# Moving and dropping the points at which GpSimd waits for VectorE while it scatters the edges of a graph

## The chip, the core and the metric

The kernel runs on one core of a Trainium2 chip. The metric is the device time of one execution in microseconds (us), lower is better. The kernel before takes 8104.89 us, the median of 3 runs (8100.04 to 8139.46). One more thing to keep in mind: the profile below was taken of the slowest of those three runs.

Engines are named as in the profile: PE is TensorE (PEld its weight load), DVE is VectorE, ACT is ScalarE, POOL is GpSimd, SP is SyncE. A small q behind the name, as in SPq, means the engine's own instruction queue.

## The reference, cut to what matters

Four graph layers run one after the other on 6250 nodes with 64 features and 206,250 directed edges, sorted by destination. Each is followed by a residual sum and a layer norm.

```python
edge_index = jnp.stack([src, dst])
x = _layernorm(x + _L0_gnn_ref(x, edge_weight, edge_weight_n2, ..., src, dst), axis=-1)
x = _layernorm(x + _L1_gnn_ref(x, edge_index, edge_attr_32, ...), axis=-1)
x = _layernorm(x + _L2_gnn_ref(x, edge_index, ...), axis=-1)
x = _layernorm(x + _L3_gnn_ref(x, edge_index, edge_attr_32, ...), axis=-1)

def _spmm(w, src, dst, h, n):
    return jax.ops.segment_sum(w[:, None] * h[src], dst, num_segments=n)
h_low = relu(_spmm(w_low, src, dst, x @ W_low, n))     # layer 0, and the same with w_high
seg_sum = segment_sum(edge_attr, row, num_segments=N)  # layer 1, with a maximum and a count too
```

Layers 0 and 1 need, for each edge, the features of its source and the edge's own 32 attributes, summed by destination or by source. The change lies in the stage that prepares this.

## The kernel before, in words

`build` runs `setup`, then `placing`, `grouping`, the rest of layer 0, and layers 1 to 3. Only `placing` is touched (lines 231 to 624).

`placing` takes the edges in NBK = 51 blocks of 4096 (128 partitions x 32 columns; the columns are c = 0 to 31). For each block it works out to which row of a table in DRAM, `pay_d`, each edge's record of 36 words goes. The table has one grid cell for each source node and block. An edge that finds its cell free goes there, the others go to a list of seconds. Then POOL scatters the records, one column of 128 rows for each call of `indirect_dma_start` (line 349), 32 calls for a block. Two blocks later the grid of a block is loaded back (line 311), and its messages are multiplied and summed into windows of 128 destinations.

The work is a pipeline over blocks, with three buffers of each kind (index j, block modulo 3). The first three blocks are written out, the other 48 run in a loop of 16 turns (`over_thirds`). All engines have the same loop and meet by semaphores alone. In stage b

- DVE compares the edges' numbers with a row of numbers (`hots(b)`, lines 501 to 506), adds up the window of block b-3 (`close_window`, 584 to 587), reads the loaded grid of block b-2 (`open_grid`, 551 to 560), and then makes the messages of block b-2 in NS = 7 parts u = 0 to 6 (`messages`, 565 to 572). Ahead of part 4 stands `ranks(b)` (512 to 522), ahead of part 6 `places(b)` (526 to 547), whose last instruction, L547, writes the row numbers of block b for POOL. `close_grid` (575 to 578) ends the stage.
- PE counts edges of block b in four batches (`counts`, 428 and 432), looks numbers up (`lookups`, 443), makes two totals (449, 450), and multiplies the messages of block b-2 part by part (`spread`, 457 to 462). Part 0 stands between batches 1 and 2, part 1 between batches 2 and 3, the others behind the lookups.
- ACT copies the end of each batch (376, 377), the running counts (382), and widens the marks of each part (370). At the end of its stage it issues three DMAs that clear other tables (398 to 400).
- SP loads a row, the edges' records and the fill of block b's grid (317 to 323), and then, when all 32 scatters of block b-2 have landed, the grid of block b-2 (311).
- POOL waits for block b's row numbers and issues its 32 scatters. Behind some of the columns it waits for a part of the messages: the table `behind` (line 338) says that ahead of column c it waits until `val_ready` has counted `(b - 1) * NS + behind[c]` parts. These are the parts of block b-1, which DVE makes in stage b+1.

Further waits on which the argument rests: part u waits in DVE for `sub_done` of part u-2 from PE (line 564), because the two buffers alternate. ACT's copy of batch t waits for PE's `batch_ready`. PE's part u waits for ACT's marks of part u.

Of the kernel before, what the change touches and what calls it, by code (L numbers as in the profile page):

```python
# [76 lines left out]
def over_thirds(eng, blocks, body):  # L77
    for b in range(3):
        body(b, 0, b)
    with eng.Fori(1, blocks // 3) as i:  # L80
        for j in range(3):
            body(i * 3 + j, i, j)
# [148 lines left out]
def placing(nc, z, k, a):  # L231
# [3 lines left out]
    with ExitStack() as ctx:  # L235
# [67 lines left out]
        with nc.Block() as block:  # L303
            @block.sync
            def _(sp):
                def load_grid(b, i, j):
                    sp.wait_ge(rows_out[j], i * (CB * 16) + CB * 16)
                    sp.sem_inc(starts, 1)
                    sp.wait_ge(grid_used, b + 1)
                    sp.sem_inc(starts, 1)  # L310
                    sp.dma_start(grid[j][:, :, :].rearrange("p s w -> p (s w)"),
                                 gv[at(b)].rearrange("b l w -> (b l) w")).then_inc(grid_in[j], 16)

                def stage(b, i, j):
                    wait(sp, lo_hot_ready, b)
                    sp.sem_inc(starts, 1)
                    sp.dma_start(lo_row[:, :], a["lo_d"][at(b), :].to_broadcast([P, BE])).then_inc(lo_in, 16)
                    wait(sp, rows_out[j], i * (CB * 16))
                    sp.sem_inc(starts, 1)
                    sp.dma_start(row[j][:, :, :].rearrange("p c w -> p (c w)"),  # L320
                                 a["pay"][at(b)].rearrange("b p w -> (b p) w")).then_inc(row_in[j], 16)
                    sp.dma_start(gv[at(b)].rearrange("b l w -> (b l) w"), fg).then_inc(filled[j], 16)
                    sp.dma_start(sv[at(b)].rearrange("b p w -> (b p) w"), fs).then_inc(filled[j], 16)
                    two_back(load_grid, b, i, j)

                over_thirds(sp, NBK, stage)
                load_grid(NBK - 2, NBK // 3 - 1, 1)
                load_grid(NBK - 1, NBK // 3 - 1, 2)
                for j in range(3):
                    sp.wait_ge(rows_out[j], NBK // 3 * (CB * 16))  # L330
                lv = sec_view(z, a)
                for j in range(3):
                    sp.dma_start(k.row[j][:, :, :].rearrange("p c w -> p (c w)"), lv[j]).then_inc(k.row_in[j], 16)
                sp.wait_ge(starts, 4 * NBK)

            @block.gpsimd
            def _(pool):
                behind = {17: 1, 20: 3, 23: 4, 26: 5, 29: 7}

                def stage(b, i, j):  # L340
                    pool.wait_ge(filled[j], i * 32 + 32)
                    pool.wait_ge(row_in[j], i * 16 + 16)
                    pool.wait_ge(place_ready, b + 1)
                    pool.sem_inc(k.pool_steps, 1)
                    for c in range(CB):
                        if c in behind and not (isinstance(b, int) and b < 1):
                            pool.wait_ge(val_ready, (b - 1) * NS + behind[c])
                            pool.sem_inc(k.pool_steps, 1)
                        pool.indirect_dma_start(a["pay_d"][:, :], bass.IndirectOffsetOnAxis(ap=place[j][:, c:c + 1], axis=0),  # L349
                                                row[j][:, c, :], None).then_inc(rows_out[j], 16)  # L350

                over_thirds(pool, NBK, stage)
                pool.wait_ge(lo_hot_ready, NBK)
                for j in range(3):
                    pool.wait_ge(k.row_in[j], 16)
                    for c in range(SC):
                        gather_listed(pool, k, a, j, c)
# [357 lines left out]
def gather_listed(pool, k, a, j, c):  # L715
    pool.indirect_dma_start(k.xs[j][:, c, :], None, a["x"][:, :],  # L716
                            bass.IndirectOffsetOnAxis(ap=k.row[j][:, c, AT_SRC:AT_SRC + 1].bitcast(i32), axis=0)
                            ).then_inc(k.x_in[j], 16)
# [2379 lines left out]
```

## Time and profile before

| | us |
|---|---|
| median of three runs | 8104.89 |
| the profiled execution's own time | 8139.46 |
| its span in the profile | 8137.8 |
| `placing`, the 32 x 51 scatters, first to last | 91.0 to 2897.4 |

The whole span has PE busy 63%, PEld 53%, DVE 57%, ACT 19% and POOL 54%. In the stretch of `placing` no engine is near full: it is a ring of waits between POOL, DVE, PE and ACT, and it has to be read from the times at which one engine lets another go. The rows that do so stand below. In a row of the timeline the number in brackets is the time for which the engine was idle before this instruction, and behind the arrow what ended it. "remote" stands where a semaphore's update ended the wait and no instruction of this core ended at that moment; "issue" where the profile shows no wait.

### The profile page before, as it was taken

Reading aid. Unit: us, or ns where it says so; the run is one execution under the profiler, and the core shown is the slowest. Engines: PE = TensorE matmul, PEld = TensorE weight load, DVE = VectorE, ACT = ScalarE, POOL = GpSimd, SP = SyncE. Lnnn points to the kernel's source line nnn. Section 1 sums busy time; section 2 is a strip of 40 time slices with the busy share of each in tenths; the row PEclk is TensorE's granted clock in tenths of the full one; section 3 lists DMA queues with packets and bytes.
Section 4 is the critical chain, followed back from the end, with each engine's and each line's share of the span. In section 5 each row is a group of like instructions: output and inputs, shape, how many; then the busy total and the mean of one; then the engine's idle time right before and its main releaser. Section 6 shows DMA issues by size and latency. Waiting matters only on the chain. (4 is left out here: it accounts for less than half of the span.)

```text
span 8137.8 us, 135968 instructions
## 1 busy us (share of the span) xinstructions
PE 5140.9 (63%) x47718; PEld 4318.4 (53%) x47719; DVE 4606.7 (57%) x8883; ACT 1556.5 (19%) x3166; POOL 4394.8 (54%) x4199
## 2 busy tenths in 40 slices
PE   2555555555555532235555567999995878778776
PEld 1433434434334422223455446999995666666665
DVE  4555555555555534445555465666665666666665
ACT  1111111111111110001111141000002333333332
POOL 3666565566566555552455554555552555555552
PEclk7677767766776766665666666999997888889887
DMA  4333233233233211111000130111113333333332
GB/s 132 112 126 126 100 123 124 102 123 126 100 123 126 86 44 28 28 29 13 21 22 22 26 120 21 27 26 26 26 25 90 95 100 95 99 98 100 95 96 52
DMA packets 303354, 621.11 MB, mean 76 GB/s; under 512 B 153436, under 2 KB 229902, under 8 KB 285521
## 3 DMA queue, kind: packets, MB, share of 16 engines
q1 hardware_dynamic: 153693, 405.75, 14.4%
q0 software_dynamic: 133216, 116.93, 6.6%
q10 hardware_dynamic: 15994, 92.31, 3.2%
q8 instruction: 297, 4.87, 0.2%
q14 instruction: 154, 1.26, 0.0%
HBM read 547.78 MB, written 235.06 MB: 96 GB/s over the span
## 5 line engine op out<-in xcount | busy, mean ns | idle before, releaser
L349 POOL DMA_INDIRECT pay_d<-row,place x1632 | 1711.9, 1049 | 1184.7 <-DVEq L572 646.0
L462 PE MATMUL win<-onehot,val 128*128 128x128 f32 x4998 | 881.9, 346 | 444.7 <-issue 233.4
L462 PEld LDWEIGHTS win<-onehot,val 128*128 128x128 f32 x4998 | 804.4, 251 | 628.7 <-issue 317.9
L2032 PE MATMUL g_win<-g_hot,y_part 128*128 128x128 bf16 x14994 | 867.8, 220 | 21.0 <-issue 11.4
L2012 POOL DMA_INDIRECT g_x<-xg_d,g_row x459 | 579.2, 1262 | 539.7 <-PE g_win L2032 413.0
L2032 PEld LDWEIGHTS g_win<-g_hot,y_part 128*128 128x128 bf16 x14994 | 847.1, 98 | 34.1 <-issue 17.2
L2534 POOL DMA_INDIRECT m_from_src<-from_src_d,m_row x459 | 515.4, 1123 | 630.6 <-PE m_pre L2570 430.7
L565 DVE TENSOR_TENSOR hot<-near_dve,drel 128x896 bf16<-128x896 bf16 x357 | 222.6, 624 | 1017.4 <-remote 746.3
L716 POOL DMA_INDIRECT lo_row_and_x<-in_x,r_row x459 | 436.9, 952 | 423.6 <-PEq L839 238.6
L1275 POOL DMA_INDIRECT sorted_d<-s_row,s_place x459 | 439.5, 958 | 333.8 <-DVE s_place L1391 145.4
L2537 POOL DMA_INDIRECT m_from_dst<-from_dst_d,m_row x459 | 518.8, 1130 | 139.9 <-issue 134.4
L832 PE MATMUL r_win<-r_onehot,r_val 128*128 128x160 f32 x918 | 212.6, 411 | 559.5 <-DVEq L856 551.3
L432 PE MATMUL pair<-hot_hi,hot_lo 128*128 128x392 bf16 (+3 forms) x1632 | 301.0, 350 | 409.2 <-DVE hot_hi L503 384.9
L832 PEld LDWEIGHTS r_win<-r_onehot,r_val 128*128 128x128 f32 x918 | 197.6, 278 | 584.1 <-DVEq L856 567.4
L2570 PEld LDWEIGHTS m_pre<-m_q_win,m_hot_t 128*128 128x128 bf16 x7497 | 358.6, 103 | 258.1 <-issue 191.7
L2570 PE MATMUL m_pre<-m_q_win,m_hot_t 128*128 128x64 bf16 x7497 | 401.5, 200 | 136.3 <-issue 135.5
L432 PEld LDWEIGHTS pair<-hot_hi,hot_lo 128*128 128x128 bf16 x1632 | 203.0, 131 | 535.8 <-issue 236.7
L2566 PE MATMUL m_pre<-m_w_four,m_ea_t 96*128 96x192 f32 (+1 forms) x1428 | 468.7, 409 | 16.7 <-issue 16.2
L370 ACT ACTIVATE onehot<-hot 128x896 f32<-128x896 bf16 x357 | 333.9, 951 | 669.3 <-DVE hot L565 612.7
L2711 DVE TENSOR_TENSOR m_hid<-m_pre,p_nodes 128x448 f32<-128x448 f32 x357 | 221.9, 622 | 404.0 <-remote 201.6
L2081 DVE TENSOR_TENSOR g_hot<-iota,g_drel 128x896 bf16<-128x896 f32 x364 | 374.5, 1087 | 110.9 <-PE g_win L2032 102.9
L2587 PE MATMUL m_win<-m_hot,m_parts 128*128 128x128 bf16 x2499 | 343.4, 229 | 68.1 <-DVE m_parts L2723 44.7
(455 smaller groups left out, 10646.9 us busy)
## 6 DMA issues: line engine op xcount, KB each, us to landing
m_hot_t<-drow_d SPq DMA_DIRECT2D x52, 1568.0 KB
scan_d<-in_none ACTq DMA_DIRECT2D x51, 1034.2 KB
lo_row_and_x<-lo_d SPq DMA_DIRECT2D x51, 1024.0 KB
m_grid<-pay_d SPq DMA_DIRECT2D x52, 882.0 KB
pay_d<-in_fill SPq DMA_DIRECT2D x51, 882.0 KB
grid<-pay_d SPq DMA_DIRECT2D x51, 882.0 KB
pay_d<-in_fill SPq DMA_DIRECT2D x51, 648.0 KB
sorted_d<-in_none ACTq DMA_DIRECT2D x51, 581.8 KB
```

The source lines that it names most:

```text
L349: pool.indirect_dma_start(a["pay_d"][:, :], bass.IndirectOffsetOnAxis(ap=place[j][:, c:c + 1], axis=0), row[j][:, c, :], None).then_inc(ro ...
L432: last = mm(pair[h][:, q, c * NT:BK * NT].rearrange("p (n s) -> p n s", s=NT), hot_lo[:, e, :], hot_hi[:, e, 0:NT].unsqueeze(1).to_broadca ...
L462: last = mm(win[:, :], val[u % 2][:, s, :], onehot[u % 2][:, s, :], start=(u == 0 and s == 0), stop=(u == NS - 1 and s == SUB - 1))
L716: pool.indirect_dma_start(k.xs[j][:, c, :], None, a["x"][:, :], bass.IndirectOffsetOnAxis(ap=k.row[j][:, c, AT_SRC:AT_SRC + 1].bitcast(i32 ...
L832: mm(win[j][:, :], val[j][:, c, :], onehot[j][:, c, :], start=(c == 0), stop=(c == SC - 1))
L1275: pool.indirect_dma_start(a["sorted_d"][:, :], bass.IndirectOffsetOnAxis(ap=place[j][:, c:c + 1], axis=0), row[j][:, c, :], None).then_inc ...
L2012: pool.indirect_dma_start(xs[j][:, c, :], None, a["xg_d"][:, :], bass.IndirectOffsetOnAxis(ap=row[j][:, c, AT_SRC:AT_SRC + 1].bitcast(i32) ...
L2032: last = mm(win[:, h, 0:W], k.y[q][:, t, h * P:(h + 1) * P], hot[u][:, s, :], start=(t == 0 and q == 0), stop=(t == NT - 1 and q == 2))
L2534: pool.indirect_dma_start(ps_x[j][:, c, :], None, a["from_src_d"][:, :], bass.IndirectOffsetOnAxis(ap=row[j][:, c, AT_SRC:AT_SRC + 1].bitc ...
L2537: pool.indirect_dma_start(qs_x[j][:, c, :], None, a["from_dst_d"][:, :], bass.IndirectOffsetOnAxis(ap=row[j][:, c, AT_DST:AT_DST + 1].bitc ...
L2566: mm(out[:, first * D:(first + size) * D], ea_t[u % 2][0:size * F, o:o + P], w_four[0:size * F, 0:size * D], start=True, stop=False)
L2570: last = mm(out[:, s * D:(s + 1) * D], hot_t[j][:, (u * SUB + s) * P:(u * SUB + s + 1) * P], q_win[j][:, q * D:(q + 1) * D], start=False, ...
```

## The change

The table `behind` of `placing` gets one entry less, and the others move three columns back:

```diff
@@ -335,7 +335,7 @@
 
             @block.gpsimd
             def _(pool):
-                behind = {17: 1, 20: 3, 23: 4, 26: 5, 29: 7}
+                behind = {20: 1, 23: 3, 26: 4, 29: 5}
 
                 def stage(b, i, j):
                     pool.wait_ge(filled[j], i * 32 + 32)
```

Before, POOL waits ahead of columns 17, 20, 23, 26 and 29 for 1, 3, 4, 5 and 7 parts. Now it waits ahead of columns 20, 23, 26 and 29 for 1, 3, 4 and 5 parts, and for all seven nowhere. The calls are the same 32 in the same order; PE, DVE, ACT and SP have the same instructions in the same order as before.

On POOL, in the loop, for the block with buffer 1 (`place_ready`, `filled1` and `row_in1` say that the row numbers are made, the grid is filled and the records are loaded; `val_ready` counts message parts; L347 and L343 are the waits' own register work):

```order
 L343 REGISTER_ALU [waits row_in1,filled1]
 L349 DMA pay_d<-row,place 554880x36 [waits place_ready]
-L349 DMA pay_d<-row,place 554880x36 x16
+L349 DMA pay_d<-row,place 554880x36 x19
 L347 ISA
-L349 DMA pay_d<-row,place 554880x36 [waits val_ready]
-L349 DMA pay_d<-row,place 554880x36 x2
-L347 REGISTER_ALU
 L349 DMA pay_d<-row,place 554880x36 [waits val_ready]
 L349 DMA pay_d<-row,place 554880x36 x2
```

The first wait for a part now stands behind 20 calls instead of 17, and one group of three calls with its wait is gone. The blocks with buffers 0 and 2 read alike.

## Rows read from the trace of the kernel before

**Rows 1.** Costliest groups: busy, mean ns of one, idle before and its releaser.

```profile
L349 POOL DMA_INDIRECT pay_d<-row,place x1632 | 1711.9, 1049 | 1184.7 <-DVEq L572 646.0
```

**Rows 2.** Busy time by stretch: PE, PEld, DVE, ACT, POOL, clock, DMA.

```profile
90.00:2900.00 2810.00, 1493.11 (x9150) 1115.18 (x9150) 1509.29 (x2650) 445.09 (x800) 1711.87 (x1632) 0.71 0.32 114
```

**Rows 3.** Waits of DVE from 90 to 2900: total us, times, longest.

```profile
DVE hot L565 <- remote: 736.0, 52, 18.8
DVE hot L565 <- PE win L462: 212.6, 57, 25.6
DVE dst_f L551 <- DMA grid<-pay_d: 123.2, 49, 6.2
```

**Rows 4.** Waits of POOL from 90 to 2900.

```profile
POOL pay_d L349 <- DVEq L572: 646.0, 154, 13.9
```

**Rows 5.** Timeline of POOL, 1605 to 1668: start, duration, instruction, idle before.

```profile
1605.94 0.97 POOL L349 DMA_INDIRECT pay_d<-row,place  x1 [0.31 <-issue]
1612.47 0.97 POOL L349 DMA_INDIRECT pay_d<-row,place  x1 [5.56 <-DVEq L572]
...
1619.12 0.96 POOL L349 DMA_INDIRECT pay_d<-row,place  x1 [3.14 <-DVEq L572]
...
1626.59 1.90 POOL L349 DMA_INDIRECT pay_d<-row,place  x1 [3.97 <-DVEq L572]
1628.80 0.97 POOL L349 DMA_INDIRECT pay_d<-row,place  x1 [0.31 <-issue]
1630.07 2.04 POOL L349 DMA_INDIRECT pay_d<-row,place  x1 [0.30 <-issue]
...
1661.15 0.96 POOL L349 DMA_INDIRECT pay_d<-row,place  x1 [0.30 <-issue]
1667.78 0.96 POOL L349 DMA_INDIRECT pay_d<-row,place  x1 [5.67 <-DVEq L572]
```

**Rows 6.** Timeline of DVE, 1609 to 1666.

```profile
1609.94 0.63 DVE L565 TENSOR_TENSOR hot<-near_dve,drel 128x896 bf16<-128x896 bf16 x1 [15.27 <-remote]
...
1623.95 0.19 DVE L547 TENSOR_TENSOR place<-away,pos 128x32 int32<-128x32 f32 x1
...
1625.13 0.61 DVE L570 TENSOR_TENSOR val<-x_nodes,near_dve 128x448 f32<-128x448 f32 x1
1625.87 1.79 DVE L575 TENSOR_TENSOR p_nodes<-grid,p_nodes 128x1568 f32<-128x1568 f32 x1
...
1629.47 1.79 DVE L578 TENSOR_TENSOR p_nodes<-p_nodes,tmp 128x1568 f32<-128x1568 f32 x1
...
1640.15 0.34 DVE L551 CAST dst_f<-grid 128x49 f32<-128x49 int32 x1 [3.04 <-DMA grid<-pay_d]
...
1647.95 0.61 DVE L570 TENSOR_TENSOR val<-x_nodes,near_dve 128x448 f32<-128x448 f32 x1
1665.25 0.62 DVE L565 TENSOR_TENSOR hot<-near_dve,drel 128x896 bf16<-128x896 bf16 x1 [16.69 <-remote]
```

**Rows 7.** Timeline of PE and ACT around three copies, and PE's part 1.

```profile
1581.78 1.67 PE L432 MATMUL pair<-hot_hi,hot_lo 128*128 128x392 bf16 x8
1583.49 0.21 ACT L376 ACTIVATE last_b<-pair 128x49 bf16<-128x49 f32 x1 [1.97 <-PE pair L432]
1592.43 0.99 PE L432 MATMUL pair<-hot_hi,hot_lo 128*128 128x392 bf16 x8
1598.67 0.21 ACT L376 ACTIVATE last_b<-pair 128x49 bf16<-128x49 f32 x1 [9.86 <-remote]
1601.74 1.31 PE L462 MATMUL win<-onehot,val 128*128 128x128 f32 x6
```

**Rows 8.** The same copy of ACT in another block, and POOL there.

```profile
1549.04 0.96 POOL L349 DMA_INDIRECT pay_d<-row,place  x1 [0.30 <-issue]
1550.51 0.21 ACT L376 ACTIVATE last_b<-pair 128x49 bf16<-128x49 f32 x1 [20.33 <-remote]
1557.64 0.97 POOL L349 DMA_INDIRECT pay_d<-row,place  x1 [7.64 <-DVEq L572]
```

**Rows 9.** Issue of a grid's load and of the clearing DMAs.

```profile
1625.38 0.84 ACTq L398 DMA_DIRECT2D sorted_d<-in_none  x1
1635.47 0.34 SPq L311 DMA_DIRECT2D grid<-pay_d  x1
```

**Rows 10.** The last block: POOL's last wait, and DVE's wait for its grid.

```profile
2893.89 1.91 POOL L349 DMA_INDIRECT pay_d<-row,place  x1 [1.71 <-DVEq L572]
2905.30 0.20 DVE L551 CAST dst_f<-grid 128x49 f32<-128x49 int32 x1 [5.47 <-DMA grid<-pay_d]
```

## The prediction, made before the changed kernel was run

> **What bounds the kernel now.** The page comes first. Its costliest group is the scatter of L349, 1632 calls, with 646.0 us of idle time ended by DVE's L572, which is exactly the wait that the change touches [rows 1]. Next the busy time of this stretch: of 2810 us POOL is busy 1711.87, DVE 1509.29, PE 1493.11 [rows 2]. Nobody is full, so the stretch is a ring of waits, and I read who lets whom go.
>
> DVE's longest wait is part 3 of the messages, ended by a "remote" update, 736.0 us in 52 times [rows 3]. The releaser should be PE's `sub_done`. In the block of rows 7 PE's part 1 ends at 1601.74 + 1.31 = 1603.05, yet DVE starts at 1609.94, 6.9 us later [rows 6]. PE's signal is held. The same shows at ACT: early in a run of scatters its copy starts at 1583.49, 0.04 us after PE's batch ends (1581.78 + 1.67), but later in that run it starts at 1598.67, 5.25 us after PE's end (1592.43 + 0.99) [rows 7].
>
> When is the held signal let go? POOL's last call before its pause ends at 1605.94 + 0.97 = 1606.91; DVE goes on at 1609.94, 3.03 us into the pause. In the next block POOL stops at 1661.15 + 0.96 = 1662.11 and DVE goes on at 1665.25, after 3.14 us [rows 5, 6]. So in both blocks PE's signal comes through only when POOL has stopped for about 3.1 us. POOL in turn stops only because it waits for that very part (column 23, four parts). That closes the ring: the length of a block is set by where POOL pauses, and by what it must wait for before its next long run.
>
> In the trace I count, for each of blocks 2 to 49, a pause ahead of columns 23, 26 and 29 and none ahead of 17 and 20: three a block, about 150 of the 154 waits [rows 4]. The block of rows 5 runs from 1606.91 to 1662.11, 55.20 us:
> - 5.56 us pause, three calls, 3.14 us pause, three calls: to 1626.59 it is 19.68 us.
> - then 26 calls in one go (columns 29 to 31, and 0 to 22 of the next block), 1626.59 to 1662.11, 35.52 us, three of them lengthened by DVE's instructions.
>
> **The change part by part.** Column 17's wait goes, and column 20 waits for one part instead of three. Neither ever made POOL idle, so both cost and give nothing. Column 23 now waits for three parts. The third is made at 1647.95 + 0.61 = 1648.56 [rows 6]; column 23 will be called some 8 us after that, by the sum below (three calls before 1606.91 + 53.6), so it does not pause either. The cover of that 8 us is the quick release of PE's part 0; were it held as well, this would be the pause.
>
> Column 26 takes over the wait for four parts and with it the long pause. The signal still comes 3.1 us after the stop, so I keep 5.56 us. Column 29 takes over the wait for five parts, 6.65 us after column 26 (1619.12 - 1612.47), since DVE's parts 3 and 4 lie so far apart whatever POOL does. So column 29 is called at 5.56 + 6.65 = 12.21 us after the stop, and its three calls end at 12.21 + 3 x 0.97 + 2 x 0.30 = 15.7.
>
> What is late next is `place_ready` of the following block, since the wait for seven parts is gone. L547 ends at 1624.14, and part 4's wait ended at 1619.12: 5.02 us. With the 0.85 us that POOL needs from DVE's end to its call (1625.13 + 0.61 = 1625.74 to 1626.59) [rows 5, 6], column 0 starts at 12.21 + 5.02 + 0.85 = 18.08. Then again 26 calls in one go (columns 0 to 25) with the same three long ones: 35.52 us. A block is 53.6 us instead of 55.2. The difference is simply part 6 end minus L547 end, 1625.74 - 1624.14 = 1.60 us, and I find this same distance in all 48 blocks.
>
> The scatters of a block now end earlier: before, column 31 ended at 1630.07 + 2.04 = 1632.11 and SP issued the grid's load at 1635.47. Now the last call ends at 1606.91 + 15.7 = 1622.6, and the load goes out near 1626, beside ACT's clearing DMAs (1625.38) [rows 9]. It took 4.7 us to DVE's L551 before, and DVE would be ready for it at 1637.1 (3.04 us before 1640.15). There are 11 us for it, enough even at twice the time. So DVE's wait for the grid, 123.2 us in 49 times, 2.5 each [rows 3], goes. I give it no gain: the two parts before the hold come 2.5 us sooner, and then DVE waits for part 3, which POOL's pause releases. That wait is what is late next. At the least it brings nothing, at the most its whole 2.5 us a block.
>
> The end of the stage: the last block paused 1.71 us at column 29, and DVE then waited 5.47 us for its grid [rows 10]. The pause for five parts moves back there by three calls (3.8 us) and the release with it. Of the 5.47 us I expect 1 to 3 to be won.
>
> Sum: 48 x 1.60 = 77, and about 3 for the end: 80 us. The profiled execution's 8139.46 becomes about 8060; from the median of 8104.89 it is **8025 us**, the profiled execution being the slowest of the three. Bounds of the unshown: the pause ahead of column 0, 2.4 us (15.7 to 18.1), may not clear what POOL has queued as 3.14 and 3.97 did. Below it costs nothing, above it costs what the slower rival says.
>
> Two rules of the Trainium skill, SBUF — State Buffer, section "SBUF: two separate sides". It says that on the engine side only the port pair shared by DVE and GpSimd causes contention, and that PE and ACT never wait for anyone. By that alone POOL's run could hold back nothing of PE's, and the long pause would not exist, before or after. The rows disagree (6.9 us held, let go 3.1 us after the stop), and I go by them. The same section says that the pair is an exclusive lock: whoever starts first has it for its whole instruction. POOL's calls do take 1.90 and 2.04 us where DVE's L575 and L578 run, against 0.97 otherwise. But L578 starts at 1629.47, within the call of 1628.80 to 1629.77, and keeps its 1.79 us, so the lock shows in one direction only. If calls of columns 0 to 2, now ahead of those instructions, did block DVE, it would lose up to 3 us of slack that it has before part 3, and the sum would stay.
>
> **The rivals.**
> - *The hold comes sooner and the change is slower.* POOL's 26 calls now start after a short pause of 2.4 us. If that does not clear its queue, PE's batches 1 and 2 (14 and 20 us into the run) are held earlier and longer. One block prices it: where batch 2 was held until POOL stopped, the pause ahead of column 23 was 7.64 us instead of 5.56 [rows 8], and I saw 9.0 and 8.1 in two other blocks. That is 2.1 to 3.4 us more a block against 1.6 won, if it holds in nearly every block instead of 3 of 48: 24 to 86 us slower, about 8160. From half the blocks on the gain is nearly gone. For it speaks that PE's signals are all held from about 26 us into a run; against it that the total of L450 and part 5's signal come through at once in the short runs of three calls.
> - *No change.* Something else spans a block, so that POOL starting 1.6 us sooner only waits that much longer ahead of column 26. The held signals would have to come at a time fixed by DVE and PE, not by POOL's stop. The two blocks (3.03 and 3.14) speak against it. Time 8105, down to 8070 if half arrives.
> - *A larger gain.* DVE's parts 0 and 1 come 2.5 us sooner and the signals slip through before the hold sets in. Then both terms count: 48 x (1.6 + 2.5) = 197, 7908 us. Part 1 of PE would still end some 25 us into the run, where all are held, so it is unlikely.
>
> **How the numbers follow.** Forecast 0.62 (own range 8005 to 8050), no change 0.15, slower 0.16, larger gain 0.07. What can be told from no change is 0.5%, 40 us. Faster by more than that: the forecast nearly whole, the larger gain: 0.66. Within: no change and the edges: 0.19. Slower: 0.15. The range reaches from 7985 to 8125: below it lies most of the larger gain, above it most of the slower rival.
>
> **What would show it.** POOL pauses ahead of columns 26, 29 and 0, with about 5.6, 3.1 and 2.4 us, and none ahead of 20 and 23; the run between the stop and the next stop is 53.6 us; DVE's part 3 starts 3.1 us after POOL stops; DVE's wait for the grid is gone; its waits on "remote" stay as large or grow by the 2.5 us. It is wrong if column 23 pauses, if the pause ahead of 26 is over 7 us as a rule, or if the signal comes before the stop.

## The result, and the profile after

The change made the kernel slower on the chip of the prediction, chip A: 8156.83 us (median of 19 runs, 8135.45 to 8179.01) against 8108.16 (19 runs, 8077.98 to 8139.46), ratio 1.0055 [1.0044, 1.0065]. Forecast were 8025 us. On three other chips the same change was 0.4 to 0.9% faster, and on one it did nothing; that is told below.

The profiled execution of after took 8125.93 us, the lowest of its own, where that of before was the highest of its own. So the two spans (8137.8 and 8124.3) can't be set against each other as they stand. The stretch of `placing` can: its scatters run from 94.5 to 2943.9, 2849.4 us, against 2808.4 before. That is 41 us more, near the 48.7 between the medians. One pair of profiles can't share out such a difference to the microsecond, though: the part behind `placing`, which is the same program in both, took 5238 us in the one profile and 5180 in the other. The page's group of the scatters, then the busy times of the stretch:

```profile
L349 POOL DMA_INDIRECT pay_d<-row,place x1632 | 1732.9, 1062 | 1208.1 <-DVEq L572 539.6
```

```profile
90.00:2945.00 2855.00, 1455.75 (x9133) 1073.68 (x9134) 1505.67 (x2656) 440.15 (x800) 1732.89 (x1632) 0.69 0.32 112
```

They answer to [rows 1, 2]: the instructions are the same, POOL's calls take 21 us more (some are stretched for longer), and the idle time ahead of them 23. Then the waits of POOL, DVE and ACT in that stretch (total us, times, longest):

```profile
POOL pay_d L349 <- DVEq L572: 539.6, 116, 13.5
POOL pay_d L349 <- DVE place L547: 129.0, 50, 3.2
```

```profile
DVE hot L565 <- remote: 633.0, 54, 18.8
DVE prod L512 <- remote: 266.6, 30, 13.5
DVE hot L565 <- PE win L462: 168.4, 104, 29.0
```

```profile
ACT last_f L377 <- remote: 784.0, 45, 21.4
ACT last_b L376 <- remote: 258.1, 21, 51.8
```

POOL waits for messages less often, 116 times instead of 154 [rows 4], and newly 50 times for the row numbers, 2.6 us each. DVE's wait for the grid, 123.2 us [rows 3], is gone from the list. But L512, the instruction behind the lookups, now waits 30 times for a "remote" update, 8.9 us each. That wait was not in the forecast, and the number 30 leads on: so many blocks are of another kind.

Call a block's length the time from its column 0 to the next block's, and a run the calls of POOL between two pauses. Over blocks 2 to 49, in us:

| | blocks | mean |
|---|---|---|
| before | 48 | 55.3 |
| after, all | 48 | 56.25 |
| after, **short**: pauses ahead of 26, 29 and 0 | 18 | 53.7 |
| after, **slipped**: at most 3.0 ahead of 26, 8.5 or more ahead of 29 | 30 | 57.8 |

The short block is the forecast one. POOL, blocks 29 and 30:

```profile
1747.65 0.97 POOL L349 DMA_INDIRECT pay_d<-row,place  x1 [0.30 <-issue]
1754.17 0.97 POOL L349 DMA_INDIRECT pay_d<-row,place  x1 [5.55 <-DVEq L572]
...
1760.82 0.97 POOL L349 DMA_INDIRECT pay_d<-row,place  x1 [3.14 <-DVEq L572]
...
1766.29 0.97 POOL L349 DMA_INDIRECT pay_d<-row,place  x1 [1.95 <-DVE place L547]
```

and DVE's part 3 in it:

```profile
1751.64 0.62 DVE L565 TENSOR_TENSOR hot<-near_dve,drel 128x896 bf16<-128x896 bf16 x1 [15.27 <-remote]
```

POOL stops at 1748.62, DVE goes on 3.02 us later, POOL waits 5.55, 3.14 and 1.95 us; column 0 starts 17.7 us after the stop (forecast 18.08). This block, from 1712.99 to 1766.29, takes 53.3 us.

The slipped block, here block 28, is another cycle:

```profile
1654.88 0.96 POOL L349 DMA_INDIRECT pay_d<-row,place  x1 [1.88 <-DVE place L547]
...
1666.94 0.21 DVE L551 CAST dst_f<-grid 128x49 f32<-128x49 int32 x1
...
1673.97 0.95 PE L432 MATMUL pair<-hot_hi,hot_lo 128*128 128x392 bf16 x8
...
1675.39 0.22 ACT L376 ACTIVATE last_b<-pair 128x49 bf16<-128x49 f32 x1 [4.92 <-PE pair L432]
...
1676.60 1.83 PE L462 MATMUL win<-onehot,val 128*128 128x128 f32 x14 [1.21 <-issue]
...
1686.72 0.62 DVE L565 TENSOR_TENSOR hot<-near_dve,drel 128x896 bf16<-128x896 bf16 x1 [11.12 <-remote]
...
1693.71 0.97 POOL L349 DMA_INDIRECT pay_d<-row,place  x1 [0.30 <-issue]
...
1698.06 0.97 DVE L512 TENSOR_TENSOR prod<-pair,hot_hi 128x784 f32<-128x784 f32 x1 [9.65 <-remote]
...
1706.48 0.97 POOL L349 DMA_INDIRECT pay_d<-row,place  x1 [11.80 <-DVEq L572]
```

A signal of PE is held when its semaphore's update comes over 1 us after the end of the matmul that gives it. PE's batch 2 ends at 1674.92, and ACT copies it 0.47 us later: its signal is hardly held. Part 1 therefore ends at 1678.43 and its signal comes at 1686.72, held 8.3 us but let go while POOL still runs. Part 3 is made before column 26, so POOL does not stop there. It stops at column 29 (1694.68), and what is held by then lies earlier in the stage: the lookups' signal, which reaches DVE's L512 at 1698.06, 3.4 us after that stop. From there DVE has ranks and two parts to do before part 5 is counted: 11.8 us of pause instead of 5.6, behind a run of 29 calls instead of 26. A block is 58.1 us.

### The profile page after: what moved, and what is told of

It reads as the page before. It is cut to its first block and busy times, and to the rows that moved or that the text cites. A ratio compares the mean times of both kernels' runs of the same rounds, so it can differ in the third digit from the quotient of the medians.

```text
span 8124.3 us, 135870 instructions
## 1 busy us (share of the span) xinstructions
PE 5066.6 (62%) x47718; PEld 4254.5 (52%) x47719; DVE 4609.9 (57%) x8883; ACT 1551.5 (19%) x3166; POOL 4420.1 (54%) x4199
## 3 DMA queue, kind: packets, MB, share of 16 engines
q1 hardware_dynamic: 153693, 405.75, 14.6%
## 5 line engine op out<-in xcount | busy, mean ns | idle before, releaser
L349 POOL DMA_INDIRECT pay_d<-row,place x1632 | 1732.9, 1062 | 1208.1 <-DVEq L572 539.6
L462 PE MATMUL win<-onehot,val 128*128 128x128 f32 x4998 | 849.8, 337 | 271.7 <-issue 156.4
L462 PEld LDWEIGHTS win<-onehot,val 128*128 128x128 f32 x4998 | 770.5, 242 | 468.3 <-issue 277.2
L565 DVE TENSOR_TENSOR hot<-near_dve,drel 128x896 bf16<-128x896 bf16 x357 | 222.7, 624 | 937.0 <-remote 633.0
L443 PE MATMUL pair<-upto,lo_hot 128*128 128x49 bf16 x1632 | 96.1, 202 | 624.3 <-ACT upto L382 502.8
```

The costliest lines, as they stand in the source:

```text
L462: last = mm(win[:, :], val[u % 2][:, s, :], onehot[u % 2][:, s, :], start=(u == 0 and s == 0), stop=(u == NS - 1 and s == SUB - 1))
```

## The experiments

Seven chips were used: A for the result, B to G below. On A, C, E and F PE's signals are held; on B, D and G they are not, and there all kernels take about 6650 us, but for the one of e4, which takes 6870. The counts of held signals compare PE's ends with the times of its semaphore updates, as far as both are in the trace.

**Chip B: late grid, last wait gone, last wait kept, waits for landed scatters.** The first takes back the only thing that comes sooner for DVE (its diff is against after), the next two are halves of the change:

```diff
+                    sp.wait_ge(lo_hot_ready, b + 3)   # e1: SP, ahead of the grid's load of block b
-                behind = {17: 1, 20: 3, 23: 4, 26: 5, 29: 7}
+                behind = {17: 1, 20: 3, 23: 4, 26: 5}     # e2
+                behind = {20: 1, 23: 3, 26: 4, 29: 7}     # e3
-                            pool.wait_ge(val_ready, (b - 1) * NS + behind[c])
+                            pool.wait_ge(rows_out[j], i * (CB * 16) + c * 16)   # e4: c is 11 or 22
```

> The changed kernel, with one wait more: SP issues the grid's load only when DVE has made the marks of that stage (lo_hot_ready), about where it went out before the change. Theory A (the grid's early load let DVE make parts 0 and 1 some 2.5 us sooner, so PE's batch 2 signals before the hold sets in, part 1's signal slips through inside the run, POOL does not pause ahead of column 26, runs 29 calls on end and pauses 11.8 us ahead of column 29): with the load late again all blocks are of the short kind, 53.3 to 53.6 us, no pause over 7 us ahead of column 29, time about 8030. Rival B (the three calls more before column 26 are enough for the signal to slip, wherever the grid's load stands): the mixture of blocks of 53.3 and 58.1 us stays, time 8150 or more.

> The kernel before with the last wait alone taken out: waits ahead of columns 17, 20, 23, 26 for 1, 3, 4, 5 parts. POOL's run then begins with column 26 and has 29 calls. If a run's length does not matter and PE's signals come 3.1 us after POOL stops: 5.6 + 3.1 us of pauses and 32 calls, 51.6 us a block, time about 7940. Theory A, which counts the hold from the start of a run (about 20 us), says that it now begins 7.5 us sooner for DVE and PE: batch 1 or part 0 is held, POOL stops ahead of column 20, or the long pause grows to over 8 us; 55 to 60 us a block, time 8100 to 8350.

> The shift alone: waits ahead of columns 20, 23, 26, 29 for 1, 3, 4, 7 parts. POOL starts its run of 29 calls (columns 29 to 25) when part 6 is made, as before. By the prediction's sum: 5.6 us ahead of column 26, then 10.2 us ahead of 29, and 39.3 us of calls, 59 us a block, time about 8290. Theory A: the grid's load goes out late as before, DVE is not early, so the signals slip in few blocks, and 8290 stands; where they slip, the pause ahead of 29 grows to 19 us and the block to 62, up to 8430.

> The kernel before without any wait for message parts; instead POOL waits ahead of columns 11 and 22 until all scatters of its block so far have landed. If the hold is a matter of POOL's own unbroken calls and ends when they have landed, whatever DVE does: pauses of 2.3 to 3.3 us, no run above 11 calls or 14 us, hardly a signal of PE held, and a block is 32 calls and two or three pauses, 49 to 51 us: 7830 to 7900. Rival (the release needs the 5.6 us pause that ends with DVE's part 3, or the hold has to do with the bulk DMAs of the stage and not with POOL's calls): signals still held 5 to 15 us, 55 us a block or more, 8100 or more.

Measured against a before of 6645.77: 1.0002 [0.9993, 1.0011], 1.0001 [0.9992, 1.001], 0.9997 [0.9988, 1.0006] and 1.0335 [1.0319, 1.0351]. They told nothing of the theories, since here none of 357 signals of L462 was held over 1 us. The waits of POOL in e1 (L349 is L352 there) and e4:

```profile
POOL pay_d L352 <- issue: 572.0, 1582, 90.0
POOL pay_d L352 <- DVEq L575: 10.7, 35, 0.3
```

```profile
POOL pay_d L349 <- DMA pay_d<-row,place: 242.2, 102, 7.5
```

No wait of the table costs anything (0.3 us is the usual step between calls), and a block is its 32 calls, 43.3 us. Waiting for landed scatters costs 2.4 us each, 47.6 us a block.

**Chips C and D: the changed kernel again, and e1 and e4 once more.**

> The changed kernel itself, once more. In the runs just made the kernel before takes 6646 us instead of 8108, all 32 scatters of a block go without a pause and a block is 43.3 us, the calls alone. Theory A with this: where PE's signals are not held, no wait of the table ever stops POOL, and the changed kernel is the same as the one before within 0.1% (ratio 0.999 to 1.001). Where they are held (the kernel before at 8108 us), it is 1.0055 again, 8150 us. Rival (the change has a cost of its own beside the hold, as more scatters on end beside the bulk DMAs): 0.3% slower or more in both.

> The changed kernel beside the next two. By its traces so far its blocks are of three kinds: short (pause of 5.6 us ahead of column 26, 53.3 us in all), slipped (no pause ahead of 26, 11.8 ahead of 29, 58.1 us) and late (9.6 ahead of 26, 57.3 us). Theory C: the ratio to the kernel before is set by how many of 48 blocks are of each kind, and this differs from chip to chip: 31 slipped gave 1.0055, 2 slipped and 13 late gave 0.993, no hold gives 1.000. So here: 53.6 us times the short ones and 58 times the others, against the blocks of the kernel before on the same chip.

> As e1, where its case could not be told since no signal was held: the changed kernel with the grid's load issued only when DVE has made the stage's marks. Theory A, where PE's signals are held: hardly a slipped block, and faster than the changed kernel on this chip by 4.5 us for each block that is slipped there. It may bring more late blocks. Rival B: as many slipped blocks as the changed kernel has. Where nothing is held: 1.000 for both.

> As e4: no wait for message parts, instead POOL waits ahead of columns 11 and 22 until its scatters so far have landed. Where nothing was held this cost 3.3%. Where PE's signals are held I expect blocks of 48 to 51 us against 55 to 57 of the kernel before, hardly a signal held over 1 us in this stage, and 200 to 400 us less, 7700 to 7900. Rival: the hold does not depend on POOL's unbroken calls, signals are still held and a block is 55 us or more.

On C the expected 1.0055 did not come; after was faster: 8136.11 against 8199.75, 0.9928 [0.9904, 0.9951], with 32 short blocks, only 3 slipped, and 13 of a third kind, **late**: over 7 us ahead of column 26. D has no hold: 0.9999 [0.9989, 1.0008], 1.0011 [1.0001, 1.0021] and 1.0331 [1.0314, 1.0348].

**Chip E: late grid, after and e4 where signals are held.**

> The changed kernel with the grid's load issued later, a third time, for a chip on which PE's signals are held. Theory A there: no or few slipped blocks (no pause ahead of column 26, over 10 us ahead of 29), about as many late ones as the changed kernel beside it; faster than that one by some 4.5 us for each slipped block that it has, so 0 to 140 us. Rival B: as many slipped blocks as the changed kernel. Where nothing is held: 1.000.

> The changed kernel beside it on the same chip. Theory C: its ratio follows from its kinds of blocks: short 53.3 us, slipped 58.1, late 57.3. Between 0.99 and 1.006 where signals are held, 1.000 where they are not.

> Pauses of POOL until its own scatters have landed, ahead of columns 11 and 22, in place of all waits for parts. Where signals are held: blocks of 48 to 51 us, hardly a signal of this stage held over 1 us, 7700 to 7900 us. Rival (the hold does not come from POOL's unbroken calls): 55 us a block or more. Where nothing is held: 1.033 once more.

Before took 8215.42. After: 0.9915 [0.9883, 0.9947], 32 short, 12 late, 4 slipped. Late grid: 0.9974 [0.9955, 0.9992], 30 short, 18 late, none slipped; its median is 46 us above that of after, where 18 us below was expected. DVE's wait for the grid is back (e9, L551 is L554 there):

```profile
DVE dst_f L554 <- DMA grid<-pay_d: 190.4, 49, 4.9
```

That no block slips agrees with the theory that the sooner grid is a condition of the slip, but 4 slipped blocks against none is thin, and it was not run on chip A, where slipped blocks are the rule; there this cause is argued and not shown. Without the sooner grid batch 2 stands 23.8 us into the run instead of 20.2, is held longer, and more blocks are late. The waits for landed scatters gave 1.001 [0.9996, 1.0024] and blocks of 56.6 us, where 48 to 51 were expected, and this list for POOL:

```profile
POOL pay_d L349 <- DMA pay_d<-row,place: 394.5, 100, 7.1
POOL pay_d L349 <- DVE place L547: 285.7, 43, 14.4
```

POOL stops there behind 10 or 11 calls as a rule, and ahead of columns 11 and 22 goes on only when they have landed. Yet of PE's signals given 6 to 18 us into a run 136 of 267 are held over 1 us; in after on the same chip they are 3 of 132. A theory by which only long unbroken runs hold signals falls.

**Chip F: before, after, and the two halves, side by side.** The kernels are before, after, and the tables of e2 and e3.

> The kernel before, unchanged, for its trace on this chip. Where PE's signals are held (before over 8100 us) I expect blocks with pauses ahead of columns 23, 26 and 29. If the change's gain on such a chip comes from its own blocks being like those of the first chip, before's blocks are 55.3 us. If before is itself longer there, as 8200 to 8215 us on two chips suggests, its mean block is about 57 us: (8200 - 8108) / 48 = 1.9 us more. Where no signal is held: no pauses and 43.3 us.

> The changed kernel beside the kernel before on one chip. If the ratio follows from the kinds of blocks: each slipped block (11 us pause ahead of column 29) costs about +2.8 us, each late one (over 7 us ahead of 26) about +2, each short one gives 1.6. With 31 short, 12 late, 4 slipped it is 55.0 us a block and 0.992 against a before of 56.4; with 18 short and 30 slipped 56.25 and 1.0055 against 55.3. Without the hold 1.000.

> Only the last wait (column 29 for seven parts) is gone, the others stay at columns 17, 20, 23 and 26. Where signals are held: by my prediction's steps column 26 goes 12.21 us after the stop, the six calls to column 31 end at 19.6, column 0 then needs no pause, and the run is 29 calls: 51.6 us a block, 48 x 3.7 = 178 us faster than before. By the slip theory a run of 29 calls is what makes the long pause (11.8 us at its end as in the slipped blocks of the changed kernel): 55 to 58 us a block, no change or up to 130 us slower. Without the hold 1.000.

> The four waits move back by three columns, but the last still waits for all seven parts. Where signals are held: with the pauses let go only by POOL's stop, column 29 goes 19.7 us after the stop and 29 calls (39.3 us) follow: 59.0 us a block, 48 x 3.7 = 178 us slower than before. If instead what counts is only that the pauses stand behind part 3, it is no slower than the changed kernel. So this and the run with only the last wait gone share the change out: the moved columns against the dropped wait. Without the hold 1.000.

| against 8175.36 | ratio | block, us |
|---|---|---|
| before | 1 | 56.00 |
| after | 0.9958 [0.994, 0.9976] | 54.77 |
| last wait gone, columns kept | 0.9844 [0.9822, 0.9865] | 53.26 |
| columns moved, last wait kept | 1.0243 [1.0219, 1.0268] | 59.65 |

This is the experiment that shares the change out, on this chip and for `placing`. Without the last wait a block is 2.7 us shorter where the columns stay, and 4.9 where they have moved. Moving the columns costs 3.6 us with the last wait and 1.5 without. (The blocks would make after 59 us faster than before, the medians say 25: in the profile of after the untouched part behind `placing` took 5275 us, in that of before 5242.) POOL's waits of the two halves, from 90 to 3130, first with the last wait gone:

```profile
POOL pay_d L349 <- DVEq L572: 519.3, 120, 10.3
```

```profile
POOL pay_d L349 <- DVEq L572: 843.1, 100, 18.7
```

And a block of each. With the last wait gone:

```profile
1772.31 0.96 POOL L349 DMA_INDIRECT pay_d<-row,place  x1 [0.30 <-issue]
1778.88 0.96 POOL L349 DMA_INDIRECT pay_d<-row,place  x1 [5.61 <-DVEq L572]
...
1785.64 0.97 POOL L349 DMA_INDIRECT pay_d<-row,place  x1 [3.26 <-DVEq L572]
1786.91 0.97 POOL L349 DMA_INDIRECT pay_d<-row,place  x1 [0.30 <-issue]
```

With the columns moved and the last wait kept:

```profile
1732.72 0.97 POOL L349 DMA_INDIRECT pay_d<-row,place  x1 [0.30 <-issue]
1740.04 0.97 POOL L349 DMA_INDIRECT pay_d<-row,place  x1 [6.35 <-DVEq L572]
...
1753.71 1.91 POOL L349 DMA_INDIRECT pay_d<-row,place  x1 [10.16 <-DVEq L572]
```

In the first, six calls from column 26 on (1785.64) cover the time in which the row numbers are made: of blocks 2 to 49 none pauses at column 0. 25 blocks with the usual two pauses take 51.6 us, the expected figure; 16 with over 7 us ahead of column 23 take 56.0, and 7 with a pause ahead of column 20 take 52.7. In the second, column 29 goes 20.0 us after the stop (1733.69; 19.7 expected) and 29 calls follow. So the ring of the prediction gives the second's mean block within 0.7 us (59.65 against 59.0), and of the first the usual block but not the mean, which is 1.7 us longer. In the medians the two are 125 us faster and 203 slower than before, where 178 was expected of each.

**Chip G: e2's table, one wait, none.** The tables are {17: 1, 20: 3, 23: 4, 26: 5}, {23: 4} and {}.

> Only the last wait gone, on another chip. Where signals are held: short blocks 51.6 us (pauses 5.6 ahead of column 23 and 3.1 ahead of 26), about a third of them longer by some 4 us, 0.984 to 0.986 as before. Without the hold: no pauses from this table, 43.3 us a block and 1.000.

> One wait is left: column 23 for four parts; those ahead of columns 17, 20, 26 and 29 are gone. Where signals are held, by the ring as I have it: pause 5.56, then nine calls to column 31 end at 16.7, column 0 goes at 18.1, 23 calls with three long ones end at 49.8: 49.8 us a block, 264 us faster than before, 0.968. Rival: part 4 and the batches behind it are let go only by a pause, so that the missing pause ahead of column 26 comes back ahead of column 0, longer: 55 us or more, no gain over the kernel with four waits (0.984). Without the hold 1.000.

> The table is empty: POOL waits for nothing but each block's row numbers. Where signals are held it stops only there, behind 32 calls (42.5 us); part 3, part 4 and the row numbers must then come after the stop: 3.1 + 6.65 + about 8 more us, 60 us a block and 1.03 to 1.04. If the signals come through after all without a pause, 50 us or less and 0.96 to 0.97. Without the hold 1.000.

No hold here either: 0.9995 [0.9986, 1.0005], 0.9998 [0.9988, 1.0007], 1.0001 [0.9991, 1.001] against 6646.69, 43.4 us a block. Whether fewer waits would do where signals are held stays open. The stretch of e16, and DVE's waits in it:

```profile
90.00:2300.00 2210.00, 1278.04 (x9151) 951.02 (x9151) 1511.47 (x2661) 445.24 (x800) 1710.09 (x1627) 0.76 0.41 145
```

```profile
DVE dst_f L551 <- DMA grid<-pay_d: 305.2, 50, 25.1
DVE hot L565 <- PE win L462: 219.7, 103, 3.2
```

DVE and POOL are as busy as before on chip A [rows 2]; "remote" is not among these waits of L565 at all.

**Why the sign differs.** In the traces of after, the blocks sort themselves by one number: for how long the signal of PE's batch 2 is held. It stands 18.1 to 21.7 us into the run on every one of these chips, 20.2 to 20.8 in the median.

| held | blocks on A | on C, E, F | mean block A | C, E, F |
|---|---|---|---|---|
| under 1 us | 19, all slipped | 1, slipped | 58.0 | 56.5 |
| 1 to 10 us | 19, 6 slipped | 89, 9 slipped | 54.8 | 54.2 |
| over 10 us | 1 | 44, 36 late | 53.6 | 56.6 |

(9 blocks on A and 10 elsewhere lack the record.) A late block shows it in two rows of after on chip F, ACT's copy and POOL's pause, with PE's batch 2 ended at 1695.57 + 0.95 = 1696.52:

```profile
1714.27 0.21 ACT L376 ACTIVATE last_b<-pair 128x49 bf16<-128x49 f32 x1 [21.98 <-remote]
```

```profile
1721.39 0.97 POOL L349 DMA_INDIRECT pay_d<-row,place  x1 [9.62 <-DVEq L572]
```

Held 17.7 us, until 2.5 us after POOL's stop at 1711.77. So the change wins only where the hold is neither too short nor too long, and how long it is differs by chip.

PE itself runs on while the signal is held. Its next matmul in that block starts as batch 2 ends, 17.8 us before ACT's copy:

```profile
1696.45 0.38 PE L457 MATMUL deg<-hot,ones 128*1 128x512 bf16 x1
```

The kinds are not scattered at random. They follow the block's place in the loop's turn of three blocks, that is, the buffer index j, block modulo 3:

| blocks with | on A | on C, E, F |
|---|---|---|
| j = 0 or 1 | 30 of 32 slipped, none late | 8 of 96 slipped, none late |
| j = 2 | all 16 short | 36 of 48 late, 3 slipped |
| mean hold of batch 2, j = 0, 1, 2 | 1.2, 0.5, 6.8 us | on F: 1.7, 2.0, 14.6 us |

The batch held in a block with j = 2 is the one of PE's first stage of a turn. Where it ends in the run does not explain this: on F, 20.2 to 20.4 us into the run, it is held 1.7 to 4.0 us in blocks with j = 0 or 1 and 17.7 to 18.4 us in those with j = 2. Before has it too (on A 5.8, 4.9 and 10.3 us). No run took the turn apart, so why the first stage is held longer stays open. Before knows no slipped block, since its part 3 is late for column 23 in any case, but it knows late ones: 3 on chip A and 10 on F (55.3 and 56.0 us a block). All 3 on A and 9 of the 10 on F have j = 2. That is part of why the ratio turned: before is slower on F by 67 us in the medians, of which `placing` has 35 in the profiles, and after is faster by 7.

## Why the prediction was wrong

- *The ring, with 5.56, 3.14 and about 2.4 us of pause and 53.6 us a block.* Right for the block it describes: 53.7 us in the mean of 18 of 48 blocks on A, about 53.9 in 32 or 33 of 48 on C, E and F. No block on A pauses at column 23.
- *Columns 17 and 20 cost nothing.* Right; no pause stands there in before.
- *The grid's load.* Its wait is gone as forecast. That its 2.5 us bring "no gain", since DVE then waits for a part "which POOL's pause releases", is **the step that failed**. I allowed the 2.5 us to be worth 0 to +2.5. On A they move batch 2 and part 1 to where their signals slip through, and the block changes into another kind, on average 2.5 us longer than before's instead of 1.6 shorter. 18 x 1.6 less 30 x 2.5 (57.8 - 55.3) is 46 us slower; the medians say 48.7. The count and the price of the slipped blocks are measured; that the sooner grid makes them rests on the run with the late grid, on chip E alone.
- *The signal comes only with POOL's stop.* I took it from two blocks, and wrote that a signal before the stop would make the forecast wrong. It came before the stop in 29 of the 30 slipped blocks, up to 4.2 us before, and 0.1 us behind it in the other. The trace of before could have warned: of 166 signals of PE held over 1 us in this stage 79 come while POOL still runs.
- *The larger gain.* It named the slip at 0.07, and had its sign wrong. It added two terms as if nothing else were held. But a pause that is not made at column 26 is made at column 29, and there the lookups, three steps earlier in the stage, are what is late.
- *The hold comes sooner.* It is the late block: absent in after on A, 11 to 13 of 48 on C, E and F, about 3 us each (57.2 against 53.9). There it ate about 36 us on F (11 blocks of 3.3), of some 95.
- *No change.* It is what happens on D, and with the other tables on B and G, for a reason that it did not name: no ring at all.
- *The three long calls.* The sum had POOL's calls as unchanged. They took 21 us more in `placing`, 0.4 us a block, and no run tells why.
- *Column 0 is late next.* Right in size, but its price was overlooked: the pause ahead of it is made only because the waits were moved. Left where they were, six calls lie over it, and the usual block is 51.6 on F (53.3 in the mean of all). My sum never priced the two halves apart.
- *The end.* 1 to 3 us were to be won. The last block pauses 3.99 us and DVE no longer waits for its grid, but it reads it at 2951.43, 7.6 us after the last call, where it was 5.9 before [rows 10]; 1.7 us lost:

```profile
2940.34 0.96 POOL L349 DMA_INDIRECT pay_d<-row,place  x1 [3.99 <-DVEq L572]
...
2942.89 0.97 POOL L349 DMA_INDIRECT pay_d<-row,place  x1 [0.30 <-issue]
```

```profile
2951.43 0.18 DVE L551 CAST dst_f<-grid 128x49 f32<-128x49 int32 x1
```

- *The rules of the Trainium skill* (SBUF — State Buffer, "SBUF: two separate sides"): it says that PE and ACT never wait for anyone, and it says so of the engines' ports to SBUF. I read it as if it spoke of PE's signals too. The hold is none of its matter: PE's matmuls run on while the signal is held (1696.45 above), so no row here contradicts the sentence. The exclusive lock shows in one direction in before: 49 of 50 runs of DVE's L578 start within a call of POOL, and all keep 1.79 us.

What causes the hold, and why on some chips only, stays open.

**A version that beats both.** Leaving the columns and dropping the last wait alone: 8050.08 us against 8175.36 for before and 8150.12 for after on chip F, and no change (0.9995) where nothing is held. It was run with a hold on one chip only, in 4 executions.

## What to carry to other kernels

In a ring of waits, price each half of a change apart, and ask of every step that comes sooner not only what it gains but which wait it lets the engines miss. A pause can be what releases other work: skipping it may move it to a costlier place. Where a delay varies from block to block, count the kinds of blocks in the whole trace before one block is taken for all, sort them by their place in the loop's turn, and where the gain is under 1%, try more than one chip.

## What the runs showed of the hardware

- The same kernel takes 6646 us on chips B, D and G and 8108 to 8215 us on A, C, E and F. In `placing` POOL and DVE are equally busy on both. What differs there is whether PE's semaphore updates reach ACT and DVE at once while POOL issues scatters: in e16 none of 710 on record is over 1 us late. PE's busy time and its mean granted clock differ too, 1493 us at 0.71 before on chip A against 1278 at 0.76. `placing` has 596 us of the 1496 between the two spans, the part behind it 904; that part was not looked into.
- Only PE's signals are held. Of the updates of ACT and DVE in `placing` that the traces of before and after on chip A and of after on chip F have, none comes over 0.01 us after its instruction's end.
- On the chips with a hold, the signal of batch 2, 20 us into a run, comes after anything from 0 to 19.8 us, longest behind PE's first stage of a loop's turn. What is still held when POOL stops mostly arrives 2.5 to 3.4 us later (in the median 3.1 to 3.3 in before and after). In before on chip A, of PE's signals 6 to 18 us into a run 2 of 93 were held over 1 us, 18 to 24 us into one 63 of 85.
- With runs of 10 or 11 scatters, and waits until those of columns 0 to 10 and 11 to 21 have landed, signals are held too, and sooner: 136 of 267 at 6 to 18 us (e11).
